# Four row buffers in a merge-and-route stage, earlier weight preparation, and an earlier handover from attention

## The reference

```python
# x: 4096 x 512, ctx: 3202 x 512, 8 experts, 512 -> 2048 -> 512, top 2, capacity 1280
def layer(x, ctx, ...):
    hc = layernorm(x)                            # 4096 rows
    Sim = (hc@w1)[:,None] + (ctx@w2)[None,:] + (hc*w3)@ctx.T + b_sim
    hq = softmax(Sim, axis=1) @ ctx
    pooled = softmax(max(Sim, axis=1), axis=0) @ hc      # one row of 512
    feats = concat([hc, hq, hc*hq, hc*pooled])   # 4096 x 2048
    x = x + tanh(g_x) * (feats @ W_qv + b_qv)
    xf = layernorm(x)
    gates = softmax(xf @ w_router + b_router)
    topv, topi = top_k(gates, 2)                 # position in the expert's buffer: running count
    h = gelu(buf @ w1 + b1); o = h @ w2 + b2     # buf: rows gathered per expert, capacity 1280
    return x + tanh(g_f) * weighted_scatter(o)
```

## Time and profile before

| | us |
|---|---|
| median of 3 runs (lowest, highest) | 2236.64 (2236.12, 2238.46) |
| the profiled execution | 2254.05 |
| its span, first to last instruction | 2252.3 |
| PE busy | 2172.4 (96%), 12015 matmuls |
| DVE busy | 1301.3 (58%) |
| ACT busy | 1142.2 (51%) |
| POOL busy | 145.7 (6%) |

### The profile page before, as it was taken

The page is one execution under the profiler, slowest core; times in us unless marked ns, Lnnn a source line. Parts: engine busy times, 40 slices in busy tenths (PEclk is TensorE's granted clock), DMA queues, the critical chain, the costliest instruction groups (busy, mean ns, idle before and its releaser), DMA issues.

```text
span 2252.3 us, 34528 instructions
## 1 busy us (share of the span) xinstructions
PE 2172.4 (96%) x12015; PEld 1123.7 (50%) x12015; DVE 1301.3 (58%) x2712; ACT 1142.2 (51%) x1747; POOL 145.7 (6%) x141
## 2 busy tenths in 40 slices
PE   5999999999999999999999995999999999999997
PEld 2444444444444444444455442646565565647463
DVE  7756566655555665554667665555556464646450
ACT  6765565655555655655433342625354363636260
POOL 0000000000000000000022222010101010010101
PEclk9999999999999999999999997999999999999999
DMA  9534444444444444335987762353433333343511
GB/s 250 133 86 94 111 110 104 106 111 93 92 108 109 111 97 115 87 84 120 269 232 206 186 160 50 144 128 100 103 102 98 107 93 107 93 116 117 132 35 23
DMA packets 484566, 265.91 MB, mean 118 GB/s; under 512 B 423860, under 2 KB 423988, under 8 KB 480428
## 3 DMA queue, kind: packets, MB, share of 16 engines
q1 hardware_dynamic: 473644, 244.90, 41.6%
q0 software_dynamic: 10880, 20.52, 4.8%
HBM read 97.96 MB, written 71.52 MB: 75 GB/s over the span
## 4 chain that ended last, share of the span: by engine, by line
PE 88%; DMA 4%; DVE 4%; issue 2%; ACT 1%; POOL 1%; SPq 0%; POOLq 0%; DVEq 0%; ACTq 0%
PE ps L1217 23%; PE ps L1233 22%; PE ps L2012 19%; PE ps L2027 18%; PE ps L1719 5%; DMA rows<-arena 2%; PE ps L367 1%; POOL rows L1426 1%; DMA arena<-arena 1%; DMA arena<-in_ctx 1%; DVE arena L202 0%; DMA feats<-arena 0%; DVE arena L742 0%; DMA arena<-feats 0%; ACT arena L1667 0%
## 5 line engine op out<-in xcount | busy, mean ns | idle before, releaser
L1217 PE MATMUL ps<-arena 128*128 128x512 f16 (+1 forms) x2688 | 557.0, 358 | 4.8 <-DMA arena<-arena 3.1
L1233 PE MATMUL ps<-arena 128*128 128x512 f16 x2400 | 552.9, 379 | 0.0
L2012 PE MATMUL ps<-arena 128*128 128x320 f16 x3072 | 421.1, 300 | 12.2 <-DMA arena<-rows 12.2
L2027 PE MATMUL ps<-arena 128*128 128x512 f16 x1920 | 415.7, 379 | 0.0
L1217 PEld LDWEIGHTS ps<-arena 128*128 128x128 f16 x2688 | 250.1, 98 | 285.5 <-issue 4.9
L1233 PEld LDWEIGHTS ps<-arena 128*128 128x128 f16 x2400 | 233.6, 98 | 275.7
L2012 PEld LDWEIGHTS ps<-arena 128*128 128x128 f16 x3072 | 301.5, 98 | 131.5 <-DMA arena<-rows 12.2
L1038 ACT ACTIVATE arena<-ps,arena 128x512 f32<-128x512 f32 (+1 forms) x224 | 163.4, 731 | 389.6 <-PE ps L1217 389.5
L2027 PEld LDWEIGHTS ps<-arena 128*128 128x128 f16 x1920 | 187.9, 98 | 225.2
L758 DVE TENSOR_REDUCE arena<-arena 128x1 f32<-128x512 f32 (+1 forms) x224 | 139.9, 626 | 192.5 <-ACT arena L1038 191.7
L771 DVE SCALAR_TENSOR_TENSOR arena<-arena 128x512 f16<-128x512 f32 x192 | 144.1, 751 | 182.4 <-ACT arena L1059 182.4
(11 more groups left out here) (245 smaller groups left out, 1380.3 us busy)
## 6 DMA issues: line engine op xcount, KB each, us to landing
arena<-in_L_ffn_w SPq DMA_DIRECT2D x64, 1024.0 KB, 10.2
feats<-arena SPq DMA_DIRECT2D x48, 512.0 KB, 2.8
arena<-in_x SPq DMA_DIRECT2D x32, 512.0 KB, 3.6
rows<-arena SPq DMA_DIRECT2D x13, 774.0 KB, 3.7
out<-arena SPq DMA_DIRECT2D x16, 512.0 KB, 3.0
arena<-in_ctx SPq DMA_DIRECT2D x6, 1024.0 KB, 13.4
arena<-arena SPq DMA_TRANSPOSE x276, 3.1
arena<-in_L_xattn_W_qv SPq DMA_DIRECT2D x4, 1024.0 KB, 7.9
```

What stands on the lines that cost most here:

```text
L1217: mm = pe.matmul(out, qT[:, q, s * KD + k, :], ctxT[:, r * KD + k, a:z], start=(k == 0 and s + r == 0), stop=(k == KD - 1 and s == 1))
L1233: mm = pe.matmul(psO[q], turned, ctxN[:, j, r, :], start=(j + s + r == 0), stop=False)
L2012: mm = pe.matmul(psH[:, f % 2, h, :], w1s[:, s, k * F + f * P:k * F + (f + 1) * P], XT[:, r, k, h * HALF:(h + 1) * HALF], start=(k + s + r ...
L2027: mm = pe.matmul(psO[:, t % 2, :], hT[:, f, s, t * P:(t + 1) * P], w2s[:, r, f * D:(f + 1) * D], start=(f + s + r == 0), stop=(f == KF - 1 ...
```

## The change

1. `merge_and_route` has four row buffers (`NR = 4`, block b uses b % 4), each with its own `sent` semaphore; `row_free` is gone. ACT and DVE wait for `sent[b % 4]` of block b-4; POOL waits for block b-2's scatters before it sends block b.
2. W1's maxima are in blocks 4 to 7, scales in 8, splits in 9 to 12.
3. ACT computes the high half of the rows directly from the sums x2, by a fused scale `rs` and a bias `shift` = -mean x rs, which DVE computes; DVE's xn is now only for the low half. Bias adds come at the head of DVE's body, statistics of tile 0 right after its sum, and block 15's bias in block 14.
4. In block 15 ACT's order is square root, Exp, high half, and PE's order of pieces differs a little.
5. DVE, ACT and POOL are written out for all blocks; PE's loop has four blocks instead of two.
6. The arena is cut anew: parts 0 and 1 of W_qv are loaded in the last unit but one into the queries' rows, parts 2 and 3 in the drain; ACT sums parts 0 and 1 in chunks 0 and 1 of the drain's first half, parts 2 and 3 in chunks 4 and 5. `scales` and five low parts come in chunk 1 of DVE's last half; the merge of block 0 takes chunks 4 to 11 first and 0 to 3 (the folded ones) last. Block 0's features are loaded after chunk 4's transpose of the drain's first half.

```diff
 class MergeOperands:
-        self.W = take([4 * KD, D], F32)
         self.Wt = take([FT, 2, D], F16)
+        late = take([2 * KD, D], F32)
...
+        early = take([2 * KD, D], F32)
+        self.W = [early[:, 0:KD, :], early[:, KD:2 * KD, :], late[:, 0:KD, :], late[:, KD:2 * KD, :]]
+        self.ORDER = tuple(range(KD, FT)) + tuple(range(KD))
...
 attention, sync:
+        def load_early(n):
+            if n == 0:
+                for q in range(QT):
+                    sp.wait_ge(q_turned[q], 16 * (NB - 1))
+                sp.wait_ge(row_step, RK * U)
+                sp.wait_ge(e_out, 16 * NB)
+            mg.load_weights(sp, n)
...
-                if last and 1 <= c < 5:
+                if last and c in (1, 2):
                     if c == 1:
                         sp.wait_ge(qk_done, NC * U)
-                    mg.load_weights(sp, c - 1)
+                    mg.load_weights(sp, c + 1)
...
                 if c == 4 and not first:
                     store_f(u - 3, 1)
+                if last and c == 4:
+                    load_first()
...
             if last:
-                load_first()
+                load_second()
...
+                if early and c in (1, 3):
+                    load_early(c // 2)
 attention, vector:
+                if last and i and c == 1:
+                    mg.scales(dve)
+                    for n in range(AHEAD):
+                        mg.low(dve, n)
                 if last and i and c == 2:
                     total_rows()
...
-                if last and i and c == 3:
-                    mg.scales(dve)
 attention, scalar:
-                if last and not i and c >= 4:
-                    mg.sum_part(act, c - 4)
-                if last and i and c == 0:
-                    mg.sum_part(act, 3)
+                if last and not i and c in (0, 1, 4, 5):
+                    mg.sum_part(act, c if c < 2 else c - 2)
 merge_and_route:
-    SPLITS = {5: (0, 1), 6: (2, 3), 7: (4, 5), 8: (6, 7)}
+    MAXES = {4: 0, 5: 1, 6: 2, 7: 3}
+    SCALED = 8
+    SPLITS = {9: (0, 1), 10: (2, 3), 11: (4, 5), 12: (6, 7)}
+    NR = 4
+    def earlier(b):
+        return 16 * 2 * QT * (b // NR)
 merge_and_route, gpsimd:
-        def send(n):
-            for v in range(2):
-                send_block(n, v)
-                pool.wait_ge(sent[v], 32 * QT * (n + 1))
-                pool.sem_inc(row_free[v], 1)
+        for b in range(NB - 1):
+            pool.wait_ge(r_step, RK * (b + 1))
+            if b >= 2:
+                pool.wait_ge(sent[(b - 2) % NR], earlier(b - 2) + 16 * 2 * QT)
             for q in range(QT):
-                scatter(v, q, v)
+                scatter(b % NR, q)
+            if b == SCALED - 3:
+                ew.reduce_max(pool, 0)
 merge_and_route, vector:
+            s.step(dve.scalar_tensor_tensor(out=shift, in0=mv[:, :, 0], scalar=-1.0, in1=rs, op0=ALU.mult, op1=ALU.mult))
...
+        def body(b):
+            v, n = b % 2, b // 2
             dve.wait_ge(x_loaded[v], 16 * (n + 1))
-            if routed == 2:
-                route_2_of(b - 2, v, n - 1)
-            y_part(b, v, 0, not routed)
-            if routed:
+            for q in range(QT):
+                add_bias(b, v, q)
+            if b >= 2:
+                route_2_of(b - 2)
+            y_part(b, v, 0, not b)
+            if b:
                 route_1_of(b - 1)
...
 merge_and_route, scalar:
-            act.wait_ge(row_free[v], n + 1)
-            for q in range(QT):
-                act.wait_ge(y_step, YK * b + 4 * QT + 2 + q)
-                act.copy(halves[v][:, q, 0:D], xn[:, q, :]).then_inc(hi_done, 1)
+            if b >= NR:
+                act.wait_ge(sent[r], earlier(b))
+            act.wait_ge(y_step, YK * b + YN + 2)
+            for q in range(QT):
+                act.activation(halves[r][:, q, 0:D], x2[v][:, q, :], ACT.Identity, bias=shift[:, q:q + 1],
+                               scale=rs[:, q:q + 1]).then_inc(hi_done, 1)
...
+        sd_last(0)
+        exp_of(NB - 2)
+        high_last(0)
+        copy_turned(NB - 1, 0)
+        exp_last(0)
+        sd_last(1)
+        high_last(1)
+        copy_turned(NB - 1, 1)
+        exp_last(1)
```

More of the change, by code:

```diff
@@ L549, in blank_rows, with body @@
                 .then_inc(rows_blank, 16)
-        def body(b, first=False, last=False, norms=True, loads=True, piece=None):
+        def load_early(n):
[5 more added lines that the diff above has]
+            mg.load_weights(sp, n)
+        def body(b, first=False, last=False, norms=True, loads=True, piece=None, early=False):
             u = 2 * b
@@ L989, in vector @@
             half(NB, i, last=True, norms=False)
-        for k in range(FT):
-            mg.low(dve, k)
+        for n in range(AHEAD, FT):
+            mg.low(dve, n)
         mg.router_scale(dve)
@@ L1172, in scalar @@
             half(NB, i, last=True, norms=False)
-        for k in range(FT):
-            mg.high(act, k, mg.scaled)
-            if k == 2:
+        for n in range(FT):
+            mg.high(act, n)
+            if n == 2:
                 mg.gates(act)
@@ L1329, in merge_and_route @@
     xn = take([QT, D], F32)
-    row = [take([QT, ROW], F32) for _ in range(3)]
+    row = [take([QT, ROW], F32) for _ in range(NR)]
     halves = [r.bitcast(F16) for r in row]
     xT = take([QT, 2, KD, P], F16)
-    stats, mv, sd, rs = take([QT, 6], F32), take([QT, 2], F32), take([QT], F32), take([QT], F32)
+    stats, mv = take([QT, 6], F32), take([QT, 2], F32)
+    sd, rs, shift = take([QT], F32), take([QT], F32), take([QT], F32)
     lneps = take([1], F32)
@@ L1345, in merge_and_route @@
     pk, kp, tot, away = (take([2, QT], F32) for _ in range(4))
-    dsti = [take([2, QT], U32) for _ in range(3)]
+    dsti = [take([2, QT], U32) for _ in range(NR)]
     wk, wsum, wi = take([QT, 2], F32), take([QT], F32), take([QT], F32)
@@ L1505, in route_1, with route_2 @@
             return s
-        def route_2(s, c, qs, v, exps, free, passed):
+        def route_2(s, c, qs, b, exps, passed):
             n = qs.stop - qs.start
-            info = row[v][:, qs, D:D + 4]
+            r = b % NR
+            info = row[r][:, qs, D:D + 4]
             first, last = qs.start, qs.stop - 1
@@ L1517, in route_2 @@
             s.step(dve.tensor_copy(base[:, first, :], count))
-            if free is not None:
-                dve.wait_ge(row_free[v], free)
+            if b >= NR:
+                dve.wait_ge(sent[r], earlier(b))
             s.step(dve.tensor_copy(info[:, :, 0:1].bitcast(U32).rearrange("p q o -> p (q o)"), tok[:, c]))
@@ L1671, in copy_turned, with exp_of, body, sd_last @@
             act.copy(xT[:, q].rearrange("p s k i -> p (s k) i"), psR[q]).then_inc(xt_ready, 1)
[L1673 to L1674 removed]
+        def exp_of(c):
+            act.wait_ge(r_step, RK * c + 3 + 2 * QT)
+            act.activation(ex, lgx, ACT.Exp).then_inc(e_done, 1)
+        def body(b):
+            v, r = b % 2, b % NR
+            if b:
+                for q in range(QT):
+                    copy_turned(b - 1, q)
+                exp_of(b - 1)
+            act.wait_ge(y_step, YK * b + YN)
+            act.activation(sd, mv[:, :, 1], ACT.Sqrt, bias=lneps[:, 0:1], scale=1 / LN_SCALE ** 2)\
+               .then_inc(sd_done, 1)
+            if b >= NR:
+                act.wait_ge(sent[r], earlier(b))
+            act.wait_ge(y_step, YK * b + YN + 2)
+            for q in range(QT):
+                act.activation(halves[r][:, q, 0:D], x2[v][:, q, :], ACT.Identity, bias=shift[:, q:q + 1],
+                               scale=rs[:, q:q + 1]).then_inc(hi_done, 1)
+        def sd_last(q):
+            act.wait_ge(y_step, YB + YL * q + 3)
             act.activation(sd[:, q:q + 1], mv[:, q, 1:2], ACT.Sqrt, bias=lneps[:, 0:1], scale=1 / LN_SCALE ** 2)\
                .then_inc(sd_done, 1)
[L1677 to L1678 removed]
+        def high_last(q):
+            r = (NB - 1) % NR
+            if q == 0:
+                act.wait_ge(sent[r], earlier(NB - 1))
+            act.wait_ge(y_step, YB + YL * q + 5)
+            act.activation(halves[r][:, q, 0:D], x2[1][:, q, :], ACT.Identity, bias=shift[:, q:q + 1],
+                           scale=rs[:, q:q + 1]).then_inc(hi_done, 1)
         def exp_last(q):
@@ L1864, in load_b2 @@
                 .then_inc(b2_loaded, 16)
-        for v in range(2):
-            sp.wait_ge(sent[v], 16 * rows_sent)
+        for r in sent:
+            sp.wait_ge(r, 16 * rows_sent)
         turn_rows(0)
```

280 lines of the change are left out of this document (115 added, 165 removed).

## The result

The changed kernel takes 2232.11 us (median of 12 runs, 2230.03 to 2234.6), the kernel before in the same session 2237.9 (12 runs, 2236.12 to 2241.26): ratio 0.9975, interval 0.9967 to 0.9983. It is faster, but by 5.8 us and not by 21; 2215.5 and the range 2211 to 2223 were wrong.

What follows compares the result with a forecast made beforehand. TensorE, 96% busy, was taken as the bound, leaving its waits and slow stretches to win. Gains 10.7 + 8.15 + 2.3 = 21.1 us, taking the median from 2236.64 to 2215.5 us; range 2211 to 2223.

Steps and rivals of the forecast that it cites:

- 17.4 us: Whole kernel: the difference between profiled execution and median, assumed to stay the same after the change, giving 2215.5 us.
- two blocks' beat is not enough: Merge blocks: with a W1 maximum or split in DVE's part, the circle through two row buffers exceeds two blocks' beat.
- Merge blocks 2 to 14: Middle merge blocks: four buffers remove the waits before the row transposes, gaining 10.7 us, bounds 0 and 10.7.
- The last block: Block 15: earlier rows and routing gain 8.15 us, bounds 3.8 and 10.
- 6.4, 0.7 and 1.05: Last block's gains: up to rows_last(0), between rows_last(0) and rows_last(1), and from rows_last(1) to the last destination, in us.
- table load: Last block: reload priced at 1.28 us by the profile row; the skill's 1.38 us drain would make it 2.66.
- From attention to merge: Handover: full gain 4.7 us, less new waits of 1.6 and 0.8, leaves 2.3 us, between 4.7 gain and 4 loss.
- wait before the pooled top: Handover: moved W_qv sums delay pool_rows, so PE newly waits 1.6 us, bounds 0 and 3.8.
- block 2 was 0.55 late: Merge start: block 2's features arrive behind W1's 4 MB load, a wait of 0.8 us, bounds 0 and 2.5.
- transposes behind the feature load: Handover: probability transposes queued on SP behind the 6.35 us feature load cost PE 0, bounds 0 and 3.
- Rival 1: Handover wins nothing because PE newly waits there; price 2.3 to 6.3 us, time taken at 2219 us; chance 0.16.
- Rival 2: Merge blocks: waits before the row transposes stay because DVE, not the buffers, is late; 2226.2 us; chance 0.10.

Runs made afterwards that it cites:

- high level: Sessions in which the unchanged kernel before took about 2251 us; the first profile, of the kernel before, also shows this level.
- session 3: Set of experiments on one chip; the kernel before, unchanged, profiled and timed again: 2238.29 us, profiled execution 2238.35, no ACT wait for row_free.
- low level: Sessions in which the unchanged kernel before took about 2238 us, as in the session of the result.
- W1 late: Changed kernel with W1's maxima back in blocks 6 to 9 and splits in 11 to 14: 2237.63 us, 4.4 over the changed kernel of its session.
- session 1: Set of experiments on one chip; the kernel before, unchanged, profiled and timed again: 2251.94 us, ACT waiting 19.5 us for row_free.
- session 2: Set of experiments on one chip, the same as session 5's; kernel before 2250.45 us, changed kernel 2233.26, ratio 0.9924.
- session 5: Set of experiments on the same chip as session 2; the kernel before took 2237.8 us.
- merge only: Kernel before with only the merge stage's edits: 2232.66 us, ratio 0.9921 in session 1; 2230.62 us, ratio 0.9969 in session 5.
- handover alone: Kernel before with only the edits of the attention stage and the merge's operands: 2249.8 us, ratio 0.9992 in session 1; 2237.91, 1.0004 in session 5.
- the one with POOL's loops written out: Control: kernel before with POOL's loops written out and nothing added: 2237.78 us, ratio 1.0001.
- e1_two_bufs: Changed kernel with two row buffers and a third for block 15, as before: 2263.65 us, ratio 1.0046 to the kernel before.
- the late scatters: Four POOL memsets ahead of the scatters of blocks 0 to 14: kernel before, POOL loops written out, 2281.24 us, ratio 1.0199; changed kernel 2231.74 us.

## Why the prediction was wrong

**The step that failed.** "The median of the runs is 2236.64, 17.4 lower; with the same difference, 2215.5 us." The 17.4 us were taken for a cost of profiling, common to both kernels. They were mostly the stalls of the closed circle, the very ones that the change removes: the profile was of the high level, the timed runs of the low one. The profiled execution of the kernel before in session 3 took 2238.35 us beside a median of 2238.29. Its span is 15.7 us shorter than that of the first profile: 10.7 us of it lie in merge blocks 2 to 14 and 2.8 in the last block, 1.2 ahead of the pooled top, 0.9 in the experts and 0.1 between. So 10.7 us of waits in the middle blocks, and 2.8 us of late halves in the last, were taken away from runs that didn't have them. With this went the reading that two blocks' beat is not enough for the circle once W1's maxima and splits are in it: session 3 has them in the same blocks, and ACT never waits. The doubt was at hand: where three runs lay within 2.3 us and the profiled execution 17.4 away, its stalls had to be explained before they were counted as a gain.

**Merge blocks 2 to 14: 10.7 us.** Right against the profile: twelve equal blocks, and none of the waits for row_free. Worth 0 at the low level, where the kernel before keeps 17.085 us by itself.

**The last block: 8.15 us.** Against the profile 9.2: 49.72 us from block 15 to the experts became 40.54. The terms were 6.4, 0.7 and 1.05; measured 6.75, 1.04 and 1.32. At the low level the kernel before is not so late there. PE and DVE of session 3:
```profile
1338.38 7.28 PE L1719 MATMUL ps<-arena 128*128 128x512 f16 x33
...
1389.21 10.97 PE L2012 MATMUL ps<-arena 128*128 128x320 f16 x66 [12.11 <-DMA arena<-rows]
```
```profile
1355.27 0.74 DVE L1575 SCALAR_TENSOR_TENSOR arena<-ps,arena 128x512 f32<-128x512 f32 x1
...
1366.79 0.75 DVE L1575 SCALAR_TENSOR_TENSOR arena<-ps,arena 128x512 f32<-128x512 f32 x1
```
Block 15 starts at 1342.26, rows_last(0) 13.0 us later instead of 15.7, the experts 46.95 us later: the term is 6.4 us, nearly the whole gain of the timed runs. The other 2.7 us of the first term were the late halves of the high level.

Which edit brings the 6.4 us was not separated at the low level. The splits leaving block 14 are a part of it: with W1 late rows_last(0) came 12.51 us after the block's start, against 10.50 in the changed kernel of that session.

On the table load: the row before priced it at 1.28 us with Exp 0.01 us behind. The changed kernel's profile has the square root's end at 1352.67, L1674's load 0.02 us behind it and the Exp 0.02 us behind the load's end:
```profile
1352.38 0.29 ACT L1694 ACTIVATE arena<-arena 128x1 f32<-128x1 f32 x1 [2.26 <-DVE arena L1599]
1352.69 1.28 ACT L1674 ACT_TABLE_LOAD   x1
1353.99 0.22 ACT L1674 ACTIVATE arena<-arena 128x20 f32<-128x20 f32 x1
```
The 1.38 us drain that the Trainium skill, "ScalarE: Activation LUTs", section "What ACT_TABLE_LOAD costs", adds is not seen, and the trace disagrees with it here.

**From attention to merge: 2.3 us.** Against the profile 0.9. The wait at the first merge product went (2.88), and 72 products took 15.70 us, not 17.39: 1.69 us, where the prediction had 1.85. The wait before the pooled top came to 1.34 (taken 1.6), block 2 was 0.55 late (taken 0.8). The term that was mis-sized is the transposes behind the feature load, taken at 0: SP's queue shows why 1.65 us came.
```profile
1070.14 7.30 SPq L251 DMA_TRANSPOSE arena<-feats  x1
1077.48 0.57 SPq L256 DMA_DIRECT2D arena<-in_x  x1
1078.25 1.24 SPq L535 DMA_TRANSPOSE arena<-arena  x1
```
And the slowness of the 72 products comes and goes without the handover's edits. The kernel before took 17.39 us for them in the first profile and in session 1, and 17.36 in session 3, but in session 2:
```profile
1085.56 15.70 PE L367 MATMUL ps<-arena 128*128 128x512 f16 x72 [2.03 <-DVE arena L373]
```
With the merge's edits alone (session 5) the wait stays, 3.17 us, and they take 15.70. Granted clock (last but two) from 1087 to 1096 us, in the profile of before and with merge only:
```profile
1087.00:1096.00 9.00, 8.89 (x34) 3.77 (x35) 8.79 (x20) 5.02 (x9) 0.00 (x0) 0.81 1.15 248
```
```profile
1087.00:1096.00 9.00, 8.28 (x39) 3.79 (x40) 8.83 (x20) 5.42 (x9) 0.00 (x0) 1.00 1.16 262
```
0.81 of full speed, part of the stretch at 1.2 GHz, against 2.4 throughout, both behind an idle stretch of some 3 us. Why is open. In the handover alone of session 5 the same slowness stands behind the new 3.04 us wait (the 15 products above). Without it the handover wins 2.88 and pays 3.5. From the start of the pooled top, without PE's wait for it, to the start of block 2 the changed kernel takes 57.6, 57.0 and 57.3 us in its three profiles, the kernel before 58.5, 58.6, 56.9 and 58.4 in its four, and the one with POOL's loops written out 56.3. Rival 1, which had 0.16, holds at both levels: handover only is timed at ratios 0.9992 and 1.0004.

**Sum.** 10.7 + 9.2 + 0.9, the pooled top 1.04 earlier and 0.2 in the experts: 22.0 from profile to profile. That this came near 21.1 is right for the middle blocks and the last, and in part luck: the pooled top, without its wait, comes anywhere from 1061.7 to 1063.6 us in the three profiles of the unedited changed kernel, so its 1.04 is chance and no gain. At the low level, session 3 against the changed kernel: 6.4 in the last block, 0.8 in the handover, 0.2 lost ahead of the pooled top and 0.7 in the experts, 6.3 us of span; 5.8 was timed.

**Rivals 2 and 3.** Rival 2 (DVE is late, not the buffers) fell with e1_two_bufs and the late scatters. Rival 3 asked what the remote rows are. "I read them as waits for logits, which cost nothing" was half right: DVE starts some 2 us after PE has finished the logits. They cost the middle blocks of the changed kernel nothing and its last block 1.6 us in session 2, and they go with the high level of the kernel before. The Trainium skill, "Runtime: NRT & Kernel Launch", section "Instruction fetch mechanics", has a taken branch, to a target that isn't fetched yet, as what stalls an engine's instruction fetch. These waits need no branch: the changed kernel's DVE stream is written out there and has five of them in session 2. What they are stays open.

## What to carry to other kernels

When the profiled execution and the timed runs of one kernel are further apart than its runs are among themselves, they are two behaviours of it: find the wait that only one of them has before any of its waits is counted as a gain. A circle through a buffer (fill, use, transfer, free) that fits its beat by less than a transfer's spread can cost nothing on one day and 13 us on another; what it is at risk of is found by adding a delay ahead of the transfer, and more buffers buy the steady time. A load moved ahead in a queue is paid by the transposes that are then behind it (1.65 us here).

## What the runs showed of the hardware

- One program, one chip, two sessions: 2250.5 and 2237.8 us, each steady within 0.3%. DVE's start behind PE's last logits differed with the level (0.04 and 1.89 us in one kernel). What sets this is open.
- In the changed kernel the scatters land in a median of 2.8 us when they go out ahead of SP's feature transposition, and in 4.8 when the memsets make the two overlap; the transposition goes from 9.3 to 11.8 us. The collision costs both sides.
- A delay of 2.28 us a block on POOL (four memsets by their row), an engine 6% busy, cost 43 us over 15 blocks, more than 15 x 2.28 = 34.2, though the circle passes POOL once in two blocks. From 1190 to 1300 us the scatters of that kernel land in a median of 3.3 us and the feature transpositions in 10.1 (2.7 and 8.2 in the kernel before in session 3). That a delay in a closed circle brings its transfers into worse company fits this; it was not shown alone.
- A slow stretch of TensorE, 1.7 us longer for 15 or 72 matmuls with a granted clock of 0.81 over 9 us in the profile of before, stands behind waits of 2.80 to 3.44 us in five profiles, and is absent behind others of 3.17 and 3.31 us.
